# Sparse spiking FFN with top-2 experts on one core: floors counted three groups later, router parts on POOL, more warming products, first GELU in three parts

## The reference, cut to what matters

```python
def _L0_cond_ref(inputs, initial_state):
    rates = jax.nn.relu(inputs) * DT                       # DT = 0.001
    c = initial_state[:, None, :] + jnp.cumsum(rates, axis=1)
    fl = jnp.floor(c)
    prev = jnp.concatenate([jnp.floor(initial_state)[:, None, :], fl[:, :-1, :]], axis=1)
    spikes = fl - prev
    return spikes / DT

def _L0_ffn_ref(x, router_w, w1, w2):
    logits = x_flat @ router_w.T
    probs = jax.nn.softmax(logits, axis=-1)
    top_v, top_i = jax.lax.top_k(probs, K)                 # K = 2 of E = 8
    top_v = top_v / jnp.sum(top_v, axis=-1, keepdims=True)
    for k in range(K):
        ...
        h = jax.nn.gelu(jnp.einsum('ech,ehf->ecf', expert_in, w1), approximate=False)
        y = jnp.einsum('ecf,efh->ech', h, w2)
        out = out + tok * (gate * keep)[:, None]

return x + _L0_ffn_ref(_L0_cond_ref(x, cond_1024), router_w, w1, w2)
```

## Time and profile before

| | |
|---|---|
| runs | 63.8, 63.9, 64.32 us; median 63.9 |
| profiled execution | 64.14 us, span 62.4 us |
| busy share of the span | PE 84%, PEld 49%, DVE 56%, ACT 44%, POOL 30% |
| instructions in it | PE 372, DVE 157, ACT 46, POOL 59 |
| chain that ended last | PE 59%, DMA 11%, DVE 10%, issue 6%, ACT 4%, POOL 3% |
| moved | 14.82 MB, mean 238 GB/s |

### The profile page before, as it was taken

How to read it: one execution, slowest core, us unless ns; L and a number is a source line. 1 busy time by engine, 2 the same in 40 slices (tenths; PEclk the granted TensorE clock), 3 DMA queues, 4 the chain that set the end, 5 groups by cost and what they waited for, 6 DMA issues and landing times.

```text
span 62.4 us, 1154 instructions
## 1 busy us (share of the span) xinstructions
PE 52.4 (84%) x372; PEld 30.5 (49%) x372; DVE 34.9 (56%) x157; ACT 27.5 (44%) x46; POOL 18.9 (30%) x59
## 2 busy tenths in 40 slices
PE   3999999999665679999999999999999999993000
PEld 1315255546122343334296679966796666570000
DVE  3399469994677966799889529590320034036000
ACT  0499459775256779146025003940199930000000
POOL 6799875200002170064867500000000000001830
PEclk9999999999999555555699999999999999999996
DMA  0399999999999995002679834999999999200130
GB/s 0 83 365 336 345 326 366 336 360 336 349 348 347 348 348 183 16 5 66 171 250 260 289 132 92 294 362 301 364 350 354 388 384 394 95 0 0 50 98 11
DMA packets 13545, 14.82 MB, mean 238 GB/s; under 512 B 648, under 2 KB 13040, under 8 KB 13536
## 3 DMA queue, kind: packets, MB, share of 16 engines
q1 hardware_dynamic: 12608, 12.62, 62.0%
q0 software_dynamic: 816, 2.01, 10.5%
q10 hardware_dynamic: 112, 0.07, 0.5%
HBM read 13.08 MB, written 2.36 MB: 248 GB/s over the span
## 4 chain that ended last, share of the span: by engine, by line
PE 59%; DMA 11%; DVE 10%; issue 6%; ACT 4%; POOL 3%; ACTq 1%; POOLq 0%; DVEq 0%
PE bank L710 23%; PE bank L694 12%; DMA w_got<-in_L_ffn_w_dram,w_index 7%; DMA router_rows<-in_L_ffn_router_w_dram 5%; PE bank L534 4%; POOL out_dram L522 3%; PE bank L565 3%; PE bank L555 2%; PE bank L574 2%; DVE floors L963 2%; PE bank L726 2%; PE bank L545 2%; PE bank L562 2%; ACTq L797 1%; PE bank L727 1%
## 5 line engine op out<-in xcount | busy, mean ns | idle before, releaser
L534 PE MATMUL bank<-ones_b 128*128 128x512 bf16 x33 | 14.5, 568 | 1.1 <-POOL ones_b L422 1.1
L710 PE MATMUL bank<-w_sb,spare_sb 128*64 128x256 f32 x128 | 14.7, 382 | 0.0
L710 PEld LDWEIGHTS bank<-w_sb,spare_sb 128*64 128x64 f32 x128 | 8.8, 137 | 4.5
L522 POOL DMA_INDIRECT out_dram<-floors,out_index x2 | 2.0, 1016 | 22.6 <-DVE floors L1164 22.3
L853 ACT ACTIVATE spare_sb<-bank 128x512 f32<-128x512 f32 x8 | 4.6, 592 | 8.5 <-PE bank L694 8.5
L694 PE MATMUL bank<-ev_pair,w_got 128*128 128x128 f32 x64 | 7.8, 278 | 0.1
L694 PEld LDWEIGHTS bank<-ev_pair,w_got 128*128 128x128 f32 x64 | 7.4, 192 | 0.7 <-DMA w_got<-in_L_ffn_w_dram,w_index 0.7
L1071 DVE TENSOR_SCALAR rate<-bank,pair_gate 128x256 f32<-128x256 f32 x4 | 1.9, 484 | 9.5 <-PE bank L710 9.5
L503 POOL DMA_INDIRECT w_got<-in_L_ffn_w_dram,w_index x4 | 4.1, 1023 | 5.5 <-DVE w_index L1060 4.9
L534 PEld LDWEIGHTS bank<-ones_b 128*128 128x128 bf16 x33 | 3.2, 119 | 4.4 <-issue 3.2
L812 ACT ACTIVATE x_hi<-x_sb 128x512 fp32r<-128x512 f32 x7 | 4.2, 623 | 1.5 <-DMA x_sb<-in_x_dram 1.5
(11 more groups left out here) (220 smaller groups left out, 80.2 us busy)
## 6 DMA issues: line engine op xcount, KB each, us to landing
w_sb<-in_L_ffn_w_dram SPq DMA_DIRECT2D x8, 1024.0 KB, 10.9
x_sb<-in_x_dram SPq DMA_DIRECT2D x8, 256.0 KB, 5.9
out_dram<-x_sb SPq DMA_DIRECT2D x1, 2048.0 KB, 14.0
cond<-in_cond_dram ACTq DMA_DIRECT2D x2, 32.0 KB, 2.2
w_got<-in_L_ffn_w_dram,w_index POOLq DMA_INDIRECT x4, 5.2
cond<-in_cond_dram SPq DMA_DIRECT2D x1, 32.0 KB, 1.9
x_rows<-in_x_dram,out_index POOLq DMA_INDIRECT x2, 3.7
out_dram<-floors,out_index POOLq DMA_INDIRECT x2, 2.8
```

The costliest lines, as they stand in the source:

```text
L534: nc.tensor.matmul(bank[2][:, 0:4 * P], ones_b[:, :], ones_b[:, :].unsqueeze(1).to_broadcast([P, 4, P]), start=True, stop=True)
L710: mm = nc.tensor.matmul(Y[d % 2][at, :], hT[:, d % 2, f, at], w2_sb[:, 2 * d + side, f, :], start=(f == 0), stop=(f == FC - 1))
```

## The change

- `LAG = 3`: weigh(g - 3) stands behind cumulate(g), and weigh(5), (6), (7) behind the loop. VectorE's and ScalarE's orders are rewritten to match.
- The router's five split operations move from VectorE to POOL, each behind a wait for the one before, ahead of `more_lists`. `routerT` is copied ahead of x_lo(1).
- `WARM_MID` grows from 2, 2, 2, 1, 1, 2 to 3, 6, 3, 3, 2, 3, and `WARM` from 3, 3, 3, 3 to 4, 4, 4, 6.
- GELU of pair 0 becomes three operations, over blocks 0 to 3, 4 to 5 and 6 to 7 (`FIRST_PARTS`), with hidden(0) writing them to banks 2, 3 and 4. The semaphores of the other pairs are renumbered.

```diff
+    LAG = 3
     WARM_ROUTER = 3
-    WARM = (3, 3, 3, 3)
-    WARM_MID = (2, 2, 2, 1, 1, 2)
+    WARM = (4, 4, 4, 6)
+    FIRST_PARTS = (3, 5, 7)
+    WARM_MID = (3, 6, 3, 3, 2, 3)
...
@@ POOL, behind the indirect transfer of line 487
+            pool.wait_ge(router_out, 1)
+            g.tensor_scalar(router_s[:, :, :], routerT[:, :, :], SPIKE, 0.0, ALU.mult, ALU.add).then_inc(router_parts, 1)
+            pool.wait_ge(router_parts, 1)
+            g.tensor_copy(router3[:, 0, :, :], router_s[:, :, :]).then_inc(router_parts, 1)
+            pool.wait_ge(router_parts, 2)
+            g.tensor_tensor(router_r[:, :, :], router_s[:, :, :], router3[:, 0, :, :], ALU.subtract).then_inc(router_parts, 1)
+            pool.wait_ge(router_parts, 3)
+            g.tensor_copy(router3[:, 1, :, :], router_r[:, :, :]).then_inc(router_parts, 1)
+            pool.wait_ge(router_parts, 4)
+            g.tensor_tensor(router3[:, 2, :, :], router_r[:, :, :], router3[:, 1, :, :], ALU.subtract).then_inc(router3_set, 1)
             pool.wait_ge(counts_set, 1)
@@ TensorE
             for g in range(XG):
                 cumulate(g)
-                if g:
-                    weigh(g - 1)
-            weigh(XG - 1)
+                if g >= LAG:
+                    weigh(g - LAG)
+            for g in range(XG - LAG, XG):
+                weigh(g)
             keep_warm(WARM_MID[0])
...
+            def first_bank(f):
+                n = sum(last < f for last in FIRST_PARTS)
+                i = f - (FIRST_PARTS[n - 1] + 1 if n else 0)
+                return bank[2 + n][:, i * PAIRS:(i + 1) * PAIRS]
...
                 for half in range(2):
-                    if d >= 2:
-                        pe.wait_ge(h_done, 2 * (d - 2) + half + 1)
+                    if d == 2:
+                        pe.wait_ge(h_first_done, len(FIRST_PARTS))
+                    elif d > 2:
+                        pe.wait_ge(h_done, 2 * (d - 3) + half + 1)
                     for i in range(CH):
                         f = half * CH + i
-                        mm = nc.tensor.matmul(HID[d % 2][half][:, i * PAIRS:(i + 1) * PAIRS],
-                                              w1_got[:, d, f * P:(f + 1) * P], ev_pair[:, d, :], start=True, stop=True)
-                    mm.then_inc(h_ready, 1)
+                        to = first_bank(f) if d == 0 else HID[d % 2][half][:, i * PAIRS:(i + 1) * PAIRS]
+                        mm = nc.tensor.matmul(to, w1_got[:, d, f * P:(f + 1) * P], ev_pair[:, d, :], start=True, stop=True)
+                        if d == 0 and f in FIRST_PARTS:
+                            mm.then_inc(h_first, 1)
+                    if d:
+                        mm.then_inc(h_ready, 1)
...
                 for f in range(FC):
-                    if f % CH == 0:
-                        pe.wait_ge(h_done, 2 * d + f // CH + 1)
+                    if d == 0:
+                        pe.wait_ge(h_first_done, sum(last < f for last in FIRST_PARTS) + 1)
+                    elif f % CH == 0:
+                        pe.wait_ge(h_done, 2 * (d - 1) + f // CH + 1)
@@ ScalarE
             take_rates(3)
+            take_rates(4)
             sign_floors(1)
-            take_rates(4)
             take_rates(5)
             sign_floors(3)
             take_rates(6)
...
+            def first_gelu():
+                at = 0
+                for n, last in enumerate(FIRST_PARTS):
+                    act.wait_ge(h_first, n + 1)
+                    nc.scalar.activation(hT[:, 0, at:last + 1, :].rearrange("p f n -> p (f n)"),
+                                         bank[2 + n][:, 0:(last + 1 - at) * PAIRS],
+                                         ACT.Gelu, scale=SPIKE).then_inc(h_first_done, 1)
+                    at = last + 1
@@ VectorE
             v.tensor_tensor(theta3[2 * B:, :], theta_r[2 * B:, :], theta_mid[2 * B:, :], ALU.subtract).then_inc(theta_set, 1)
-            take_rests(1)
-            take_floors(0)
-            take_rests(2)
             dve.wait_ge(router_t, 1)
             v.tensor_copy(routerT[:, :, :], bank[5][:, 0:KC * E].rearrange("p (k e) -> p k e", k=KC)).then_inc(router_out, 1)
+            take_rests(1)
+            take_rests(2)
             take_rests(3)
+            take_floors(0)
+            take_rests(4)
+            take_rests(5)
             take_floors(2)
-            take_rests(4)
...
+            take_rests(6)
+            take_rests(7)
             take_floors(4)
...
             take_floors(7)
```

More of the change, by code:

```diff
@@ L252, in adaln_ffn_kernel @@
         router3_set = sem("router3_set")
+        router_parts = sem("router_parts")
         rates = sem("rates")
@@ L314, in adaln_ffn_kernel @@
         w1_in = [sem(f"w1_in{i}") for i in range(D)]
+        h_first = sem("h_first")
+        h_first_done = sem("h_first_done")
         h_ready = sem("h_ready")
@@ L851, in gelu @@
                 for half in range(2):
-                    act.wait_ge(h_ready, 2 * d + half + 1)
+                    act.wait_ge(h_ready, 2 * (d - 1) + half + 1)
                     nc.scalar.activation(hT[:, d % 2, half * CH:(half + 1) * CH, :].rearrange("p f n -> p (f n)"),
@@ L886, in check_x @@
                                      ACT.Relu, bias=x_bound[:, 0:1], accum_out=faults[:, 0:1]).then_inc(x_seen, 1)
-            for d in range(D):
+            first_gelu()
+            for d in range(1, D):
                 gelu(d)
-                if d >= 1:
-                    round_y(d - 1)
+                round_y(d - 1)
                 if d == 2:
@@ L967, in _ @@
             v.tensor_tensor(theta3[2 * B:, :], theta_r[2 * B:, :], theta_mid[2 * B:, :], ALU.subtract).then_inc(theta_set, 1)
-            take_rests(1)
-            take_floors(0)
-            take_rests(2)
             dve.wait_ge(router_t, 1)
             v.tensor_copy(routerT[:, :, :], bank[5][:, 0:KC * E].rearrange("p (k e) -> p k e", k=KC)).then_inc(router_out, 1)
+            take_rests(1)
+            take_rests(2)
             take_rests(3)
+            take_floors(0)
+            take_rests(4)
+            take_rests(5)
             take_floors(2)
-            take_rests(4)
[L976 to L980, removed]
-            take_floors(4)
[L982 to L989, removed]
+            take_rests(6)
+            take_rests(7)
+            take_floors(4)
             take_floors(7)
```

## The result

| | before | changed |
|---|---|---|
| median of the runs | 64.06 us (6 runs, 63.8 to 64.55) | 63.23 us (6 runs, 62.86 to 63.58) |
| profiled execution, span | 64.14, 62.4 us | 63.3, 61.6 us |
| hidden(0) starts | 31.15 | 29.42 |

A forecast was written before the change was run, and what follows sets the result against it. Bound by a chain of waits: the loop's sums, a ladder of short operations, gather, then hidden and project products. Loop 1.2 plus clock 0.2 makes 1.4 us off 63.9, forecast 62.5 us; range 61.8 to 64.6.

The forecast's parts named there:

- Part 1, loop: In the loop summing x's groups, floors three groups later let weigh(7) start at 15.20 instead of 16.39; 1.2 us, bounds 0.6 to 1.3.
- POOL's parts: Router parts moved to POOL cost zero, end by 13.5, and leave VectorE's x_lo operations beside them undisturbed.
- Part 2, clock: Ten more warming products in the middle's gaps hold TensorE's full clock; 0.2 us gained, bounds 0 and 0.5.
- Part 3, warming between the maps: Six last warming products end near 29.6, before the gather at 29.7, fitting by 0.1 us; bounds 0 and +0.2.
- a sign of being wrong: Before hidden(0): it would wait for the warming products instead of the gather.
- Part 4: First GELU in three operations changes nothing, as project(0) needs block 4 only near 34.9; zero, bounds -0.1 and +0.1.
- The step that failed: Sum up to hidden(0): loop 1.2 plus clock 0.2 give 1.4 us, with everything behind it unchanged.
- the second GELU is long done: Behind hidden(0): the second GELU (33.23, 0.60 us) finishes well before project(0) needs block 4, near 34.9.
- the clock was not lost: Rivals near 20 us: clock falls and returns, 64.1 us, chance 0.20; or stays down through the maps, 67.0, 0.14.
- the rival of POOL against VectorE: In the loop, POOL's router parts hold up VectorE by at worst 1.45 us: 63.7, at half 63.2; chance 0.10.

The follow-up runs named there:

- a_two: Changed kernel's code with the first GELU in two parts (blocks 0 to 3 and 4 to 7) instead of three; 64.08 us, before 64.16.
- loop_only_2: Kernel before with only the new loop order and router parts on POOL, old warming products and GELU, on chip C; 62.32 us, before 63.66.
- after_2: The changed kernel itself, run again on chip C; 62.07 us, before 63.66.
- before_3: The kernel before, unchanged, run again with a trace on chip A; 63.86 us, ratio 0.995 to itself.
- a_oldgelu_2: Changed kernel with the first GELU of before, in two operations, on chip C; 62.02 us, before 63.66.
- a_once: Changed kernel with project(0) waiting only ahead of the first block of each GELU part, not all eight blocks; 63.17 us, before 64.16.
- after_3: The changed kernel itself, run again on chip D; 62.58 us, before 63.84.
- a_oldgelu: Changed kernel with the first GELU of before, in two operations, on chip A; 64.06 us, before 64.16.
- third set: Runs on chip C of the changed kernel, two variants with the old GELU, and the loop part alone; changed kernel 62.07 us, before 63.66.
- late_rows_old: Changed kernel with the old two-part GELU and the x_rows loads held back until y of group 0 is set; 61.98 us on chip B, before 63.71.
- a_oldgelu_3: Changed kernel with the first GELU of before, in two operations, again on chip A; 64.07 us, before 64.21.
- warm_only: Kernel before with only the new numbers of warming products (WARM and WARM_MID), on chip D; 65.39 us, before 63.84.
- b_gelu3: Kernel before with only the three-part first GELU, on chip A; 63.83 us, before 64.16.
- late_rows_old_3: Changed kernel with the old two-part GELU and x_rows loads held back until y of group 0, on chip A; 61.99 us, before 64.21.
- late_rows_3: Changed kernel with its three-part GELU and x_rows loads held back until y of group 0, on chip D; 62.28 us, before 63.84.

## Why the prediction was right or wrong

- **Part 1, loop: 1.2 us. Right.** weigh(7) started at 15.20 by forecast and at 14.76 in the result; the extra 0.44 goes with x's sooner landing. Like with like: where x landed late, 16.39 before and 15.51 in `a_two`, 0.9; where it landed early, 15.40 to 16.16 in four traces with the old order against 13.95 to 14.81 in 14 with the new one: 1.5 between the medians, 15.74 and 14.28. The forecast lies between. `loop_only_2` took 1.34 us off the median.
- **POOL's parts: zero. Right, for another reason.** They mostly ran behind the last x_lo, not beside it, since the indirect transfer ahead of them ended late: the last one ended near 14.0, not 13.5. Where the first did begin inside an x_lo, it was POOL that was drawn out (0.70 us in the result for 0.21 elsewhere), as the affine select in the earlier trace rows. The Trainium skill's rule in "SBUF — State Buffer", section "SBUF: two separate sides", that the two lock each other out for an instruction, agrees with that row; there the loser was POOL. The prediction had taken no loss for x_lo from its rows, and that was not quite right: two of the seven took 778 and 773 ns beside POOL's constants (it had named 0.75 us beside the router parts as a sign), and the seven took 708 ns on average for 684. Nor did its rows bear on the rule for two inputs: the write of spread and the cast in the earlier trace rows have one input each.
- **Part 2, clock: 0.2 us. Right.** The clock is 1.00 from 17 to 56 us in the result, and in `after_2` it falls only in the last two slices of the page; with the old warming it fell in the middle in `before_3` and `loop_only_2` as in the earlier trace rows. From weigh(7) to hidden(0) the six traces with the old numbers of warming products take 14.57 to 14.76 us and the 14 with the new ones 14.32 to 14.73: 0.2 between the medians, 14.73 and 14.52. By time it is less sharp: on chip C `a_oldgelu_2` took 62.02 and `loop_only_2` 62.32, 0.3 with ratios whose intervals overlap.
- **Part 3, warming between the maps: zero.** Right, with nothing to spare. The six products ended at 29.23 and hidden(0) waited 0.19 us more for the gather, where 0.1 had been forecast. In `a_once`, `after_2`, `a_oldgelu_2` and `after_3` hidden(0) followed the sixth product at once, which the prediction had named as a sign of being wrong; no loss shows there, as 14.32 to 14.46 us from weigh(7) to hidden(0) are the shortest of all.
- **Part 4, "Zero; bounds -0.1 and +0.1": right on C** (`after_2` 62.07, `a_oldgelu_2` 62.02), **wrong on A**, where the three parts are worth 0.9 (`a_oldgelu` 64.06, `a_once` 63.17).
- **The step that failed: "Hidden(0) starts 1.2 + 0.2 = 1.4 us earlier, and nothing behind it changes."** It was 1.73 earlier, and 0.92 of it was lost behind it to the reports of hidden(0). The step had copied the second GELU's 0.30 us of idling from the earlier trace rows, as if a report took the same time whatever else was in flight and on every chip. The slack of 1.17 us in project(0) had been taken for safe ("the second GELU is long done"); a report that is up to 3.0 us late goes through it. The delay is also longer with the change's warming products, which the sum had only as a gain: 1.4 to 1.5 us in the two late traces with the old numbers, 2.7 to 3.0 in the seven with the new ones. Like with like the change itself gives back less than 0.92: on A the kernel before already loses 0.40 in this piece (6.29 in `before_3`, 6.80 in the result). Where the reports are in time the sum stands: 1.59 us measured in the third set, 1.4 forecast.
- **The rivals.** None occurred: the clock was not lost, and POOL held up nothing that the end of the loop shows. The 0.6 us that are missing went by a mechanism that was in no rival. That 63.23 lies in the range is luck, by the width that was given to others; so is that the rival of POOL against VectorE names 63.2 at half its price.

## What to carry to other kernels

Wherever a chain is shortened, the slack of each handover behind it has to be written down with what else is then in flight, indirect transfers above all; a time of 0.3 us for a report is only known for the state in which it was seen. Transfers that nobody needs yet (x_rows here) are worth issuing behind the handovers that are on the path: `late_rows_old` took 61.98, 62.35 and 61.99 us on the three chips where it ran (B, C, A), where `a_oldgelu` took 62.02 on one and 64.07 on another. On A that is ahead of both kernels (before 64.21; the changed kernel with single waits, `a_once`, 63.17); on C the changed kernel is as good (62.07). And one chip is not enough to test a mechanism: two sets here told opposite stories.

## What was not expected of the hardware

- A report from TensorE to ScalarE came up to 3.0 us later than in the earlier trace rows (2.70 in `a_oldgelu_3`, 2.90 in `warm_only`; by the semaphore's own record 3.00 behind the product in `after_3`, 3.05 in `a_once`), on chips A and D and never on B and C, where five traces have the loads of x_rows early. In seven of the nine late traces, the result among them, the last GELU that waited for one began 3.2 to 3.4 us after the first issue of x_rows (30.74 to 33.99; 32.39 to 35.62; 30.53 to 33.73 in `after_3`; 30.96 to 34.38 in the result), within 0.1 us of its first recorded landing, in `before_3` 1.7 and in `b_gelu3` 1.9, ahead of any landing.
- The late traces carry a second mark: for the gathers of w1 and the loads of x_rows a part of the records of landing is missing. The profile then names no time to landing. The changed kernel in the result, then in `after_2`:

```profile
w_got<-in_L_ffn_w_dram,w_index POOLq DMA_INDIRECT x4
```

```profile
w_got<-in_L_ffn_w_dram,w_index POOLq DMA_INDIRECT x4, 4.7
```

  Each trace on B and C, and that of the kernel before from which the rows come, holds 473 records of semaphores set by transfers; the nine late ones hold 423 to 436, `late_rows_old_3` and `late_rows_3` on A and D 446 and 448, with their reports in time. So the result, whose chip is not named in its data, is of A's kind (426), and the earlier trace rows came from an execution of the other kind: the 0.30 us had been read where it could not show the delay.
- What holds the report is open, and so is why the chips differ. That x_rows is needed for it is shown on A (`late_rows_old_3`), supported on D. It does not cover everything: the first report in the result was 0.8 us late (31.42, where 1.19 us behind hidden(0) is 30.61), before x_rows was issued at 30.96, with the fourth gather of w1 (issued at 29.66) under way. Whether that one has the same cause was not tried. The missing records name a rival that no run tests: that the recording of the execution takes part in the delay.
- The clock fell to half in the old middle and held at full in the new one with ten more products in six gaps. Before it came back in the kernel before, TensorE had been busy for 6.81 of 6.90 us.
